# Adding the residual where the attention's output tiles are evicted, and loading one tensor less in the feed-forward stage

## The reference

```
def norm(x, t, gw, gb, bw, bb):
    g = (t @ gw.T + gb)[:, None, :]
    b = (t @ bw.T + bb)[:, None, :]
    return g * x * rsqrt(mean(x * x, -1) + 1e-6) + b

x1  = x + attention(norm(x, t, g1w, g1b, b1w, b1b), Wq, Wk, Wv, Wo)      # 16 heads of 32
x2  = x1 + silu(h @ gate_w.T) * (h @ hid_w.T) @ out_w.T                  # h = norm(x1, t, g2w, ...), 2048 hidden
out = x + x2
```

## Time and profile before

| what | value |
|---|---|
| time, median of 3 runs | 2409.89 us (2408.28 to 2412.3) |
| the profiled execution: its own time | 2412.49 us |
| its span, first to last instruction | 2410.4 us |
| mean granted TensorE clock | 0.983 |
| busy: TensorE matmul | 2284.6 us (95%) |
| busy: VectorE | 1666.5 us (69%) |
| busy: GpSimd | 1424.3 us (59%) |
| busy: ScalarE | 1310.2 us (54%) |
| moved by DMA | 209.60 MB, mean 87 GB/s |
| end of attention, start of the feed-forward program | about 1389 us |

### The profile page before, as it was taken

How to read it: one execution, slowest core, us unless ns; L and a number is a source line. 1 busy time by engine, 2 the same in 40 slices (tenths; PEclk the granted TensorE clock), 3 DMA queues, 4 the chain that set the end, 5 groups by cost and what they waited for, 6 DMA issues and landing times. The chain is left out here.

```text
span 2410.4 us, 40369 instructions
## 1 busy us (share of the span) xinstructions
PE 2284.6 (95%) x10916; PEld 1570.9 (65%) x10916; DVE 1666.5 (69%) x2740; ACT 1310.2 (54%) x2335; POOL 1424.3 (59%) x1329
## 2 busy tenths in 40 slices
PE   5999999999999999999999849999999999999999
PEld 4655447555466554475554538888888888888887
DVE  4777735776637777357766358877887788778877
ACT  3367772567753677725677444454435444544454
POOL 0399980799943998908989437603770267127611
PEclk9999999999999999999999969999999999999999
DMA  5222212221132222122221422136312631253125
GB/s 189 78 58 51 64 41 85 71 53 44 50 107 53 61 50 62 41 85 71 54 45 49 161 91 98 36 102 202 117 36 92 196 124 44 88 192 132 44 83 179
DMA packets 92656, 209.60 MB, mean 87 GB/s; under 512 B 15632, under 2 KB 15632, under 8 KB 90640
## 3 DMA queue, kind: packets, MB, share of 16 engines
q1 hardware_dynamic: 90768, 194.32, 27.1%
q10 hardware_dynamic: 576, 8.39, 0.9%
q0 software_dynamic: 1088, 4.19, 0.5%
HBM read 134.23 MB, written 19.92 MB: 64 GB/s over the span
## 5 line engine op out<-in xcount | busy, mean ns | idle before, releaser
L732 DVE TENSOR_REDUCE pmax<-bank 128x1 f32<-128x512 f32 x1024 | 652.8, 684 | 203.9 <-PE bank L974 193.9
L644 ACT ACTIVATE probs<-bank 128x512 f32<-128x512 f32 x1024 | 567.2, 602 | 288.2 <-PE bank L1077 232.0
L479 POOL TENSOR_TENSOR sums<-sums,probs 128x512 f32<-128x512 f32 x432 | 540.9, 1287 | 0.0
L1077 PE MATMUL bank<-qs,ks 128*128 128x512 f32 x1024 | 435.8, 429 | 14.1 <-ACT probs L644 11.4
L974 PE MATMUL bank<-ks,qs 96*128 96x512 f32 x1024 | 407.4, 410 | 31.2 <-DVE pmax L732 30.1
L1077 PEld LDWEIGHTS bank<-qs,ks 128*128 128x128 f32 x1024 | 192.9, 189 | 274.9 <-issue 124.4
L1637 PE MATMUL bank<-H_hi,wt_hi 128*128 128x512 f32 x896 | 350.0, 391 | 14.7 <-DVE H_lo L1492 14.6
L1651 PE MATMUL bank<-ow,aw 128*128 128x512 f32 x1536 | 358.6, 392 | 0.0
L1637 PE MATMUL bank<-H_lo,wt_hi 128*128 128x512 f32 x896 | 349.5, 390 | 0.0
L1637 PE MATMUL bank<-H_hi,wt_lo 128*128 128x512 f32 x896 | 349.5, 390 | 0.0
L1651 PEld LDWEIGHTS bank<-ow,aw 128*128 128x128 f32 x1536 | 285.7, 188 | 59.7 <-issue 1.2
(11 more groups left out here) (156 smaller groups left out, 3385.0 us busy)
## 6 DMA issues: line engine op xcount, KB each, us to landing
raw<-in_gu_w SPq DMA_DIRECT2D x66, 512.0 KB, 3.5
wo_raw<-in_out_w SPq DMA_DIRECT2D x128, 256.0 KB, 2.7
ks<-qk_hi SPq DMA_DIRECT2D x136, 128.0 KB, 2.4
qs<-qk_hi SPq DMA_DIRECT2D x264, 64.0 KB, 2.0
x<-in_x SPq DMA_DIRECT2D x10, 1024.0 KB, 5.1
ks<-qk_lo SPq DMA_DIRECT2D x68, 128.0 KB, 2.4
qs<-qk_lo SPq DMA_DIRECT2D x132, 64.0 KB, 2.0
attn_out<-yout SPq DMA_DIRECT2D x32, 256.0 KB, 2.4
```

The costliest lines, as they stand in the source:

```text
L479: nc.gpsimd.tensor_tensor(total, first, probs[:, s % 2, h, :], ALU.add) \
L644: nc.scalar.activation(probs[:, s % 2, h, :], sbank[i % SB][:], ACT.Exp, scale=SCALE).then_inc(st_done, 1)
L732: nc.vector.reduce_max(pmax[:, t, h, hf:hf + 1], mbank[n % MB][:], AX_X).then_inc(sq_done, 1)
L1077: nc.tensor.matmul(sbank[i % SB][:], ks[:, g % 2, h, s * P:(s + 1) * P], qs[:, u % 3, h, :], start=True, stop=True).then_inc(st_ready, 1)
```

## The change

The attention program adds `x` to a tile when it evicts it, so that the tensor between the programs is `x_mid` = x + attention (the reference's x1). To do this it loads 8 tiles of `x` for each batch, 256 KB each, on SP. There is no new space in SBUF for them: the tiles 0, 1, 6 and 7 go to the second slots of `qk_hi` and `qk_lo`, free when the last keys are stacked, and the tiles 2 to 5 to `sums`, free when the last denominators are done. SP waits for these two events ahead of the stores. The feed-forward program no longer loads `xr` and no longer adds; its last step is x + x_mid in place of 2x + attn.

```diff
+    def residual_place(i):
+        return qk[i % 2][:, 1, :].bitcast(F32) if i < 2 or i >= NT - 2 else sums[:, i - 2, :]
...
+        residual_loaded = [sem(f"residual_loaded{i}") for i in range(NT)]
...
+            def load_residual(b, i):
+                sp.dma_start(residual_place(i), x[b, i * P:(i + 1) * P, :]).then_inc(residual_loaded[i], 16)
...
+                for s in k_stacked:
+                    hold(sp, held, s, b * (NG * HEAD_INC) + (NG + 1) * HEAD_INC)
+                load_residual(b, 0)
+                load_residual(b, 1)
+                hold(sp, held, w_ready, MISC(b, misc_index(True, ("D", NU - 1, 1)) + 1))
+                for t in range(2, NT - 2):
+                    load_residual(b, t)
                 for t in range(NT):
 
                     hold(sp, held, sq_done, SCORES_Q(b, NU * NMAX + t + 1) + MB)
-                    sp.dma_start(attn[b, t * P:(t + 1) * P, :], yout[:, t % 2, :]).then_inc(y_stored[t % 2], 16)
+                    sp.dma_start(x_mid[b, t * P:(t + 1) * P, :], yout[:, t % 2, :]).then_inc(y_stored[t % 2], 16)
+                    if t < 2:
+                        load_residual(b, NT - 2 + t)
...
-                    nc.vector.tensor_copy(yout[:, t % 2, :], mbank[n % MB][:]).then_inc(sq_done, 1)
+                    dve.wait_ge(residual_loaded[t], b * 16 + 16)
+                    nc.vector.tensor_tensor(yout[:, t % 2, :], mbank[n % MB][:], residual_place(t), ALU.add).then_inc(sq_done, 1)
...
# feed-forward program
-                sp.dma_start(x1[:, TPH + t, :], attn[b, rows, :]).then_inc(res_loaded[t], 16)
+                sp.dma_start(x1[:, TPH + t, :], x_mid[b, rows, :]).then_inc(res_loaded[t], 16)
...
                 for hf in range(2):
-                    sp.dma_start(x1[:, TPH * hf:TPH * (hf + 1), :], tokens(attn, prepared, hf)).then_inc(x_loaded[hf], 16)
-                    sp.dma_start(xr[:, TPH * hf:TPH * (hf + 1), :], tokens(x, prepared, hf)).then_inc(x_loaded[hf], 16)
+                    sp.dma_start(x1[:, TPH * hf:TPH * (hf + 1), :], tokens(x_mid, prepared, hf)).then_inc(x_loaded[hf], 16)
...
             def square(n, t):
-                act.wait_ge(summed, n * 8 + (t + 1))
+                if not isinstance(n, int):
+                    act.wait_ge(x_loaded[t // TPH], n * 16)
...
-            def add_x(n, t):
-                if not isinstance(n, int):
-                    dve.wait_ge(x_loaded[t // TPH], n * 32)
-                nc.vector.tensor_tensor(x1[:, t, :], x1[:, t, :], xr[:, t, :], ALU.add).then_inc(summed, 1)
...
-                nc.vector.scalar_tensor_tensor(x1[:, t, :], x1[:, t, :], 2.0, x1[:, TPH + t, :], ALU.mult,
-                                               ALU.add).then_inc(res_summed, 1)
+                nc.vector.tensor_tensor(x1[:, t, :], x1[:, t, :], x1[:, TPH + t, :], ALU.add).then_inc(res_summed, 1)
...
-            for t in range(8):
-                add_x(0, t)
...
-                    if 4 <= j < 8:
-                        add_x(b + 1, 2 * (j - 4))
-                        add_x(b + 1, 2 * (j - 4) + 1)
...
# the early loads that GpSimd issues in the attention's last batch
-             for hf in range(2) for to, src in ((x1, attn), (xr, x))]
+             for hf in range(2)]
```

More of the change, by code:

```diff
@@ L223, in next_batch, with attention_program @@
     return (b + 1) % NB
-def attention_program(nc, x, cond_small, cond_in, W_in, attn, wv_dram, wo_dram, W, ffn_loads, cst, psum):
+def attention_program(nc, x, cond_small, cond_in, W_in, x_mid, wv_dram, wo_dram, W, ffn_loads, cst, psum):
     wq, wk, wo_lo = W
@@ L413, in _ @@
                         load_x(b, 1, prepared)
+                for s in k_stacked:
[5 more added lines that the diff above has]
+                    load_residual(b, t)
                 for t in range(NT):
                     hold(sp, held, sq_done, SCORES_Q(b, NU * NMAX + t + 1) + MB)
-                    sp.dma_start(attn[b, t * P:(t + 1) * P, :], yout[:, t % 2, :]).then_inc(y_stored[t % 2], 16)
+                    sp.dma_start(x_mid[b, t * P:(t + 1) * P, :], yout[:, t % 2, :]).then_inc(y_stored[t % 2], 16)
+                    if t < 2:
+                        load_residual(b, NT - 2 + t)
             for s in y_stored:
                 hold(sp, held, s, (NB * (NT // 2) + 1) * 16)
+            for s in residual_loaded:
+                hold(sp, held, s, NB * 16)
             hold(sp, held, wv_loaded, (NB + 1) * 16)
@@ L1120, with ffn_program @@
               9 * i + 8: (i, (T3,)), 9 * i + 9: (i, (T2,)), 9 * i + 10: (i, (T4,))}
-def ffn_program(nc, x, attn, gu_w, out_w, out, cst, psum):
+def ffn_program(nc, x, x_mid, gu_w, out_w, out, cst, psum):
     at = cst["at"]
@@ L1127, in ffn_program @@
     gain_now, bias_now = cst["gain_now"], cst["bias_now"]
-    x1, xr = cst["ffn_early"]
+    x1, unused = cst["ffn_early"]
     a = at("a", [P, NJ, NBLK, QB], F32, "a")
@@ L1278, in _ @@
             for i in range(2):
-                hold(sp, held, x_loaded[i], NB * 32)
+                hold(sp, held, x_loaded[i], NB * 16)
             hold(sp, held, raw_loaded[0], 16 * (NB * 6 + 1))
@@ L1330, in square @@
             def square(n, t):
-                act.wait_ge(summed, n * 8 + (t + 1))
+                if not isinstance(n, int):
+                    act.wait_ge(x_loaded[t // TPH], n * 16)
                 if t == 0 and not isinstance(n, int):
                     act.wait_ge(var_ready, n)
-                nc.scalar.activation(xr[:, t, :], x1[:, t, :], ACT.Square, accum_out=ssq[:, t:t + 1]).then_inc(sq_sum, 1)
+                nc.scalar.activation(unused[:, t, :], x1[:, t, :], ACT.Square, accum_out=ssq[:, t:t + 1]).then_inc(sq_sum, 1)
             def weight_hi(b, j, lead=False, parts=(0, 1, 2)):
@@ L1658, in condition_block @@
 def condition_block(nc, x, cond_small, cond_w, w_in, gu_w, out_w, out):
-    attn = nc.dram_tensor("attn_out", (NB, L, D), F32, kind="Internal").ap()
+    x_mid = nc.dram_tensor("x_mid", (NB, L, D), F32, kind="Internal").ap()
     wv_dram = nc.dram_tensor("wv_parts", (P, 2, KT, D), F32, kind="Internal").ap()
@@ L1707, in condition_block @@
     cst["x_first"] = [at(f"x{hf}", [P, TPH, D], F32, ("x4", "o")[hf]) for hf in range(NHALF)]
-    x1, xr = at("x1", [P, NT, D], F32, "x1"), at("xr", [P, NT, D], F32, "r1")
-    cst["ffn_early"] = x1, xr
+    x1, unused = at("x1", [P, NT, D], F32, "x1"), at("unused", [P, NT, D], F32, "r1")
+    cst["ffn_early"] = x1, unused
     assert places["x1"] >= places["ks"] + 4 * GH * L and places["r1"] + 4 * NT * D <= places["probs"]
-    early = [(to[:, TPH * hf:TPH * (hf + 1), :], src[0, hf * QB:(hf + 1) * QB, :].rearrange("(t p) d -> p t d", p=P))
-             for hf in range(2) for to, src in ((x1, attn), (xr, x))]
+    early = [(x1[:, TPH * hf:TPH * (hf + 1), :], x_mid[0, hf * QB:(hf + 1) * QB, :].rearrange("(t p) d -> p t d", p=P))
+             for hf in range(2)]
     cst["g1"], cst["b1"], cst["g2"], cst["b2"] = cst["cond"]
@@ L1720, in condition_block @@
         psum = [ctx.enter_context(nc.psum_tensor(f"bank{i}", [P, QB], F32)) for i in range(8)]
-        attention_program(nc, x, cond_small, cond_w, w_in, attn, wv_dram, wo_dram, W, early, cst, psum)
-        ffn_program(nc, x, attn, gu_w, out_w, out, cst, psum)
+        attention_program(nc, x, cond_small, cond_w, w_in, x_mid, wv_dram, wo_dram, W, early, cst, psum)
+        ffn_program(nc, x, x_mid, gu_w, out_w, out, cst, psum)
 _NORMS = ("g1", "b1", "g2", "b2")
```

1 line of the change is left out of this document (removed).

## The result

The changed kernel takes **2440.81 us** (median of 4 runs, 2436.32 to 2443.59), against 2411.10 for the kernel before in its 4 runs: ratio **1.012, 95% interval 1.0101 to 1.0139**. It is slower by 1.2%. The prediction was 2436, with a range of 2414 to 2447 and 0.87 on slower.

The account below looks back on a forecast made before the run. TensorE bounds the feed-forward loop (971.93 of 972.00 us), so the change shows at batch ends and the lead: 22.8 + 5.6 - 1.6 = +26.8 us on the profiled 2412.49, given as 2436 against the median, range 2414 to 2447.

Parts of the forecast that it names:

- The ends of batches 0, 1 and 2: End of these attention batches: tile 2 evicted late, TensorE stalls at tile 5; +7.6 us each, 22.8 in all.
- The store of tile 0: End of batch 0, SP's queue: behind four loads and beside wv, lands at 379.3; tile 2's eviction was needed by 374.3.
- A transfer behind wv: SP's queue at a batch's end: each further 256 KB transfer takes 0.77 us at 340 GB/s.
- TensorE was to be idle: At tile 5, end of batches 0 to 2: idle 5.0 us, because tile 2 is evicted that late.
- The clock: TensorE after the stall in batches 0 to 2: lower granted clock, costing another 2.8 us each.
- one long stall: Ends of batches 0 to 2: one long stall, not two, since tile 6 isn't due for 2.7 us more.
- Batch 3: End of batch 3, GpSimd's loads beside wv: tile 2 late, three tiles left instead of two; +5.6 us, bounds +2 and +10.
- The lead: Start of the feed-forward program: VectorE's eight additions go, GpSimd's first sum is faster; -1.6 us, bounds 0 and -2.
- The addition and the loop: Addition at eviction costs nothing; removed feed-forward loop additions and loads are hidden by TensorE: 0.
- rival of equal shares: Both queues get equal bytes, ends of batches: stalls of 2.7 us without clock loss, +7.9 us, 2418; chance 0.20.

Follow-up runs that it names:

- e1: Changed kernel, but SP stores tile 0 before it waits for the last denominators and loads tiles 2 to 5: 2424.26 us, ratio 1.0051.
- e2: Changed kernel without the loads of tiles 2 to 7, the store of tile 0 still behind the wait: 2424.43 us, ratio 1.005.
- e5: Changed kernel with wv fetched on SP's own queue, behind the store of tile 0 and the load of tile 6: 2438.33 us, ratio 1.0111.
- e6: Changed kernel with a place of its own for each output tile, added in place and stored from there: 2411.01 us, ratio 1.0001.
- e3: Kernel before with the feed-forward part of the change alone, x neither loaded nor added there: 2409.41 us, ratio 0.9987.
- e8: Kernel before with the eviction as an addition of something already in SBUF, no new loads and no moved store: ratio 1.0007.
- e9: Changed kernel with wv laid out in DRAM so its fetch moves rows of 2 KB in place of 16 KB: 2440.72 us, ratio 1.0125.
- e12: As e6, but wv fetched in two transfers of 1 MB, one behind the other: 2407.85 us, ratio 0.9986 to the kernel before.
- e4: Changed kernel with wv's fetch issued 3.4 us later, behind ScalarE's high part of tile 4: 2442.57 us, ratio 1.0125.

## Why the prediction was right, point by point

**The time, the sign and the mechanism were right.** The sum was +26.8 us; the medians differ by 29.7, and the ratio's interval is 24.4 to 33.5 us.

**The ends of batches 0, 1 and 2: forecast +22.8, measured +22.8** (8.06 + 6.62 + 8.15, cut to V, from the table). The parts hold too. The store of tile 0 was to land at 379.3; it landed at 379.4, in an execution whose cut is 0.6 us earlier. A transfer behind wv was to add 0.77 us; it added 0.6 to 1.1. TensorE was to be idle for 5.0 us; it was for 5.48, 4.84 and 5.98. The clock was to cost 2.8 us; counted over the pitches above 0.3 us after each stall it was 2.9, 2.3 and 2.6. There was one long stall in each batch and no second one. That the sum agrees to the last digit is luck: the three batches cost 6.6 to 8.2 us where 7.6 was forecast for each.

**Which step decides.** The prediction put it on the store of tile 0, behind the moved wait and four loads, beside wv. e1 and e2 divide it: without the moved store 3 us of each stall stay, for the load of tile 2; without the loads 2.8 us stay, for the store. Each alone is enough to be late, since each is issued with wv and lands with it; together the fifth transfer in the queue lands 3.3 to 3.5 us behind wv. e5 shows it in the other direction: with wv behind the store in the same queue, that store takes 3.6 us. And e6, which has the same bytes and no loss, shows that the volume by itself was not the matter.

**Batch 3: forecast +5.6, measured +5.4.** The place was right, the size in part by luck. TensorE resumed 16.8 us after the cut by the forecast and 17.6 in the trace (3.7 us later than in the kernel before, where 2.9 was forecast), with three tiles left in place of two. What came after made up for it: 2.5 us of clock in place of 2.8, and a last store of 2.0 us where it had taken 3.2 beside a 1 MB load of x that is gone (2.0 in e3 as well).

**The lead: forecast -1.6, measured -1.8,** and -1.4 in e3. GpSimd's first sum is back at its usual time, the counterpart of the earlier trace rows:

```profile
1418.92 0.72 POOL L1307 TENSOR_TENSOR s_lead<-raw 128x256 f32<-128x256 f32 x1 [33.88 <-DMA raw<-in_gu_w]
...
1426.02 1.66 POOL L1316 TENSOR_TENSOR inv<-var,mhalf 128x8 f32<-128x8 f32 x1
```

The Trainium skill (SBUF — State Buffer, Who interferes with whom) names the cause, a VectorE instruction with two SBUF inputs beside a GpSimd instruction that reads SBUF. The runs agree: 2.32 us beside VectorE's additions, 0.72 without them. The loads of x went with the additions, but in the kernel before these had all landed by 1388, and GpSimd's sum began at 1392.70.

**The addition and the loop: forecast 0,** measured 1.0007 (e8) and 982.8 us in either kernel (e3).

**What was not right.** The rival of equal shares was sized wrongly. It said that if both queues got equal bytes the store would land at 377.0 and the change would cost 7.9 us. e9 comes near equal shares, and the store still lands 13.0 us after wv's issue. The error is in the rate: that sum used 340 GB/s from 368.5 on, but the transfers start slowly (148 GB/s from 368 to 370 in e9), the loads of the tiles 6 and 7 and the store of tile 1 join in, and the shares are not equal even with rows of one size: from 370 to 373 wv still moved 0.70 MB and SP's queue 0.32. The chance of 0.20 for that case was thus given to a price that the chip doesn't have. And the moved wait alone, which e2 prices at over 40% of the loss (13.2 of 29.7 us), was in the sum only as a part of the queue, not as a cost that would stand with the loads gone.

The Trainium skill (DMA: Bandwidth & Descriptors, Queues, rings and completion order) has each engine take turns between queues by packets of several descriptors. The turns are there, but a turn is of one or two rows. The DMA queues of the changed kernel and of e9 between 370 and 373 us (q10 is ScalarE's, with wv; q1 is SP's): rows moved, MB, share of the 16 engines' time.

```profile
q10 hardware_dynamic: 70, 1.15, 90.7%
q1 hardware_dynamic: 55, 0.11, 9.7%
...
q10 hardware_dynamic: 342, 0.70, 67.2%
q1 hardware_dynamic: 173, 0.32, 30.5%
```

In the changed kernel a row of wv took 0.62 us (90.7% of 16 engines for 3 us, by 70) and an engine has eight of them. They began at 368.1, so no engine was done with its eight before 373, and with turns of nine or more rows none of SP's could have moved by then; 55 had. Laid end to end by start and duration, the rows of an engine alternate, mostly one of wv and one of SP's. So the measurement decides against the size of a turn that the Trainium skill gives. It also says why the small transfer lands with the large one: 256 KB in rows of 2 KB and 2 MB in rows of 16 KB are eight rows for each engine, so they run out together, and the bytes don't matter (within 0.2 us of it in e2, 0.2 behind in the changed kernel, between the halves in e12). The prediction had it that the store gets through only when the large transfer is done; its rows move in between, and only its landing is that late. The sum is the same either way.

## What to carry to other kernels

A small transfer that somebody waits for must not be in flight together with a large one, whichever queue they are on and whichever was issued first: price it as landing when the large one does, plus one step of its own data for each transfer ahead of it in its queue. That holds where both have the same number of rows; with eight times as many in the large one (e9) the first small one landed 2.2 us sooner, and fewer than in the large one's eight per engine was not run. Before a wait is put ahead of stores on a queue, ask which buffer those stores free, and who stands behind it in an engine's order; here a store issued 2.6 us later (e2, 13 us) cost as much as all the new loads with the store in its place (e1, 13 us). Work taken from engines beside a loop that TensorE fills is worth nothing, so what pays for it elsewhere must be free.

## What was not expected

**A stall of about 3 us costs the clock or doesn't.** After stalls of 3.94 us and more the lower level followed each time, for 1.6 to 3.5 us of loss. After seven stalls of 2.8 to 3.6 us (six in e1 and e2, one in e6) it followed in five, with 1.8 to 2.9 us of loss, and in two it did not. The same stall in two batches of one execution of e1:

```profile
714.48 0.77 PE L1024 MATMUL bank<-wo_hi,osplit 128*128 128x512 f32 x1 [3.55 <-DVE osplit L852]
715.04 0.63 PE L1024 MATMUL bank<-wo_lo,osplit 128*128 128x512 f32 x1
...
1049.74 0.47 PE L1024 MATMUL bank<-wo_hi,osplit 128*128 128x512 f32 x1 [3.35 <-DVE osplit L852]
1050.05 0.39 PE L1024 MATMUL bank<-wo_lo,osplit 128*128 128x512 f32 x1
```

Matmuls of 0.63 us after the first, of 0.39 after the second. A stall in this range costs its own length and, in five cases of seven here, nearly as much again.

**A store that began its issue before wv and landed with it** (e4): 11.9 us for 256 KB, the longest of batch 0 in any of these kernels. Its issue took 1.3 us; what held it is open.
